# Products with V in three blocks of columns for two units instead of two for one, and the sums copied a unit later

## What is computed

```python
scores = jnp.einsum('bhqd,bhkd->bhqk', q, k) / math.sqrt(hd)
causal = jnp.triu(jnp.ones((S, S), dtype=bool), k=1)
scores = jnp.where(causal[None, None], -jnp.inf, scores)
attn = jax.nn.softmax(scores, axis=-1)
attn_out = jnp.einsum('bhqk,bhkd->bhqd', attn, v)
```

## Time and profile before

| | |
|---|---|
| median of 3 runs | 2348.08 us (2337.51 to 2354.03) |
| the profiled execution | 2345.42 us, span 2343.7 us |
| first maximum job to last product with V | 378 to 1919 us of the span |
| first scores to last product with V | 464 to 1919 us |
| PE, DVE, ACT busy in the span | 95%, 83%, 62% |

### The profile page before, as it was taken

The page is one execution under the profiler, slowest core; times in us unless marked ns, Lnnn a source line. Parts: engine busy times, 40 slices in busy tenths (PEclk is TensorE's granted clock), DMA queues, the critical chain, the costliest instruction groups (busy, mean ns, idle before and its releaser), DMA issues. The chain is left out here.

```text
span 2343.7 us, 48214 instructions
## 1 busy us (share of the span) xinstructions
PE 2221.6 (95%) x18596; PEld 1346.0 (57%) x18596; DVE 1955.3 (83%) x3662; ACT 1460.4 (62%) x1759; POOL 216.2 (9%) x287
## 2 busy tenths in 40 slices
PE   0999997999999999999999999999999989999998
PEld 0888984444444454444444444444444438998998
DVE  8788786979989989999899989899888826777887
ACT  1444440077767777777777778778778775555443
POOL 3111111010020310000000000000000000000544
PEclk9999996589989999999999999999999999999999
DMA  5223327111110120210001111000200016443232
GB/s 141 86 95 125 121 94 144 39 34 35 34 44 17 60 62 2 66 34 12 22 11 34 34 49 55 22 14 10 31 19 8 4 37 191 154 149 103 80 99 81
DMA packets 138310, 143.67 MB, mean 61 GB/s; under 512 B 36184, under 2 KB 101336, under 8 KB 137992
## 3 DMA queue, kind: packets, MB, share of 16 engines
q1 hardware_dynamic: 134784, 132.56, 20.0%
q0 software_dynamic: 3072, 8.39, 1.1%
q10 hardware_dynamic: 288, 0.39, 0.1%
HBM read 88.17 MB, written 51.02 MB: 59 GB/s over the span
## 5 line engine op out<-in xcount | busy, mean ns | idle before, releaser
L1048 DVE TENSOR_REDUCE attn_MX<-psB 128x1 f32<-128x512 f32 (+3 forms) x2176 | 1331.9, 670 | 160.9 <-PE psB L862 98.0
L1021 ACT ACTIVATE attn_PB<-psB 128x1024 f32<-128x1024 f32 (+3 forms) x1152 | 1076.3, 954 | 383.1 <-PE psB L916 314.3
L862 PE MATMUL psB<-KS,attn_QS 52*128 52x512 f32 (+3 forms) x1152 | 331.9, 457 | 25.1 <-DMA KS<-picking_rows 16.1
L938 PE MATMUL psB<-attn_PB,V 128*32 128x256 f32 (+4 forms) x4008 | 338.6, 410 | 0.0
L938 PE MATMUL psB<-attn_PB,attn_V 128*32 128x256 f32 (+5 forms) x3552 | 320.6, 433 | 0.5 <-ACT attn_PB L1021 0.4
L916 PE MATMUL psB<-attn_QS,KS 52*128 52x512 f32 (+3 forms) x1152 | 285.1, 473 | 0.1
L862 PE MATMUL psB<-attn_KS,attn_QS 52*128 52x512 f32 (+3 forms) x1152 | 279.6, 405 | 3.1 <-DVE attn_MX L1048 1.9
L916 PE MATMUL psB<-attn_QS,attn_KS 52*128 52x512 f32 (+3 forms) x1152 | 273.6, 461 | 4.8 <-ACT attn_PB L1021 3.8
L862 PEld LDWEIGHTS psB<-KS,attn_QS 52*128 52x128 f32 x1152 | 192.7, 201 | 94.6 <-DVE attn_MX L1048 67.5
L916 PEld LDWEIGHTS psB<-attn_QS,attn_KS 52*128 52x128 f32 x1152 | 111.3, 183 | 228.3 <-issue 116.7
L916 PEld LDWEIGHTS psB<-attn_QS,KS 52*128 52x128 f32 x1152 | 114.6, 187 | 218.4 <-issue 145.8
(11 more groups left out here) (232 smaller groups left out, 3102.4 us busy)
## 6 DMA issues: line engine op xcount, KB each, us to landing
W<-in_w SPq DMA_DIRECT2D x18, 1024.0 KB, 5.4
qk_parts<-proj_PT SPq DMA_DIRECT2D x32, 512.0 KB, 2.8
attn_QS<-qk_parts SPq DMA_DIRECT2D x192, 64.0 KB
v_rows<-proj_VA SPq DMA_DIRECT2D x32, 256.0 KB, 2.0
attn_KS<-qk_parts SPq DMA_DIRECT2D x96, 64.0 KB, 2.8
KS<-qk_parts SPq DMA_DIRECT2D x90, 64.0 KB, 3.2
XN<-in_x SPq DMA_DIRECT2D x8, 512.0 KB, 7.5
rows_by_place<-proj_ZR SPq DMA_DIRECT2D x32, 128.0 KB, 2.2
```

The costliest lines, as they stand in the source:

```text
L862: mm = nc.tensor.matmul(ps[:, bank, at * width:(at + 1) * width], QS[rows, i % 4, b, j * P:(j + 1) * P], KS[w][rows, b, kc * CH:kc * CH + ...
L938: mm = nc.tensor.matmul(ps[32 * h:32 * (h + 1), PV, cols], V[w][:, kb, 32 * h:32 * (h + 1)], PB[:, u % RING, h, cols], start=(k == 0 and f ...
L1021: nc.scalar.activation(PB[:, u % RING, 2 * pair:2 * pair + 2, r * P:CH], ps[:, 2 * (s % 2):2 * (s % 2) + 2, r * P:CH], ACT.Exp, scale=HD * ...
L1048: nc.vector.tensor_reduce(MX[:, m % 4, first:first + 2 * n - 1:2, kc], ps[:, MB + off % 3, 0:n * w].rearrange("p (h n) -> p h n", h=n), AX ...
```

## The change

PE's order is now written for two units a and b together, with the two units before them (`behind`) weighed in three blocks of columns. For eight new jobs in a pair of units it is: first scores of a, 3 jobs, block one; second scores of a, 1 job, first scores of b, 1 job, block two; second scores of b, 3 jobs, block three. Blocks are cut at a third and two thirds of all columns of both units, so the middle block has a part of each unit, with its own matmuls. The last two units are weighed whole at the end. ACT copies the sums of the step before after the second unit of a step instead of after the first. In steps with only four units SP moves the rows of maxima before it stores the sums.

```diff
+                    rows_first = i + 1 < LS and len(units[i]) == TPC
+                    if rows_first:
+                        move_rows(i + 1)
                     if i > 0:
                         sp.wait_ge(ou_ready, i + 1)
                         store_sums(i - 1)
...
-                    if i + 1 < LS:
+                    if i + 1 < LS and not rows_first:
                         move_rows(i + 1)
...
-                        scores(i, k, 0)
-                        ask(done + (2 if halves else (new + 1) // 2))
-                        if halves:
-                            mid = (units[behind[0]][behind[1]][1] * P + CH) // 2
-                            weigh(*behind, 0, mid)
-                        scores(i, k, 1)
...
-                        ask(done + 4 if halves else upto[i][k])
-                        if behind is not None:
-                            weigh(*behind, mid if halves else 0, CH)
...
+                    widths = [CH - P * units[i][k][1] for i, k in two]
+                    ends = [sum(widths) * q // 3 // 16 * 16 for q in range(3)] + [sum(widths)]
+                    for (i, k), base, width in zip(two, (0, widths[0]), widths):
+                        first, last = [min(max(end - base, 0), width) for end in ends[third:third + 2]]
+                        if first < last:
+                            weigh(i, k, CH - width + first if first > 0 else 0, CH - width + last)
...
+                    share = lambda q: at + ((of_b - at) * q + 4) // 8
+                    first, second = min(share(3), of_a), max(share(5), of_a)
+                    both_scores(*a, 0)
+                    ask(first)
+                    weigh_third(behind, 0)
+                    both_scores(*a, 1)
+                    ask(of_a)
+                    both_scores(*b, 0)
+                    ask(second)
+                    weigh_third(behind, 1)
+                    both_scores(*b, 1)
+                    ask(of_b)
+                    weigh_third(behind, 2)
...
-                        if k == 0 and i > 0:
+                        if k == 1 and i > 0:
                             sums(i - 1)
```

More of the change, by code:

```diff
@@ L959, in _ @@
                             max_rows(0, 0, None, 1)
-                behind = None
+                flow = [(i, k) for i in range(LS) for k in range(len(units[i]))]
                 at = j_base[AHEAD]
@@ L968, in ask @@
                         at += 1
[L970 to L974, removed]
-                        scores(i, k, 0)
-                        ask(done + (2 if halves else (new + 1) // 2))
-                        if halves:
-                            mid = (units[behind[0]][behind[1]][1] * P + CH) // 2
-                            weigh(*behind, 0, mid)
-                        scores(i, k, 1)
-                        if k == rows_at(i) and i + 1 < LS:
-                            max_rows(i + 1, s_rows(i), s_rows(i) - 1, i + 2)
-                        ask(done + 4 if halves else upto[i][k])
-                        if behind is not None:
-                            weigh(*behind, mid if halves else 0, CH)
[L986 to L989, removed]
@@ L990, in _, with both_scores, weigh_third @@
-                weigh(*behind, 0, CH)
+                def both_scores(i, k, pair):
+                    scores(i, k, pair)
+                    if pair == 1 and k == rows_at(i) and i + 1 < LS:
+                        max_rows(i + 1, s_rows(i), s_rows(i) - 1, i + 2)
+                def weigh_third(two, third):
+                    if not two:
+                        return
+                    widths = [CH - P * units[i][k][1] for i, k in two]
[4 more added lines that the diff above has]
+                            weigh(i, k, CH - width + first if first > 0 else 0, CH - width + last)
@@ new lines, in _ @@
+                for n in range(0, len(flow), 2):
+                    a, b = flow[n:n + 2]
+                    behind = flow[max(n - 2, 0):n]
+                    of_a, of_b = upto[a[0]][a[1]], upto[b[0]][b[1]]
+                    share = lambda q: at + ((of_b - at) * q + 4) // 8
[11 more added lines that the diff above has]
+                    weigh_third(behind, 2)
+                    if a == (LS - 1, 0):
+                        transposes()
@@ L992, in _ @@
+                for i, k in flow[-2:]:
+                    weigh(i, k, 0, CH)
             @block.scalar
```

## The result

The changed kernel takes 2536.24 us (median of 4 runs, 2523.21 to 2547.78) against 2344.58 us before: a ratio of 1.082, 95% interval 1.078 to 1.086. I had forecast slower, 2480 us, with a range up to 2525. The direction was right and so was the mechanism at the joints; the size was too small by 56 us, and the next sections find what was missing. Times are medians of all runs; clocks, half-clock times and lines are those of the profiled execution.

The account below looks back on a forecast made before the run. PE sets the pace, with DVE near, and waits for banks at joints should decide: 36 + 35 + 37 + 23 = 131 us on the profiled 2345.4 us, forecast 2480 us. Its own range is 2450 to 2510, over all 2415 to 2525.

Parts of the forecast that it names:

- joint of six: Six jobs around only block three, at joints between pairs: job n waits for job n-3's reduce; 190 of 287 joints.
- The price of a joint: Full pairs cannot repeat faster than 5.49 us: 0.47 us more with eight or nine jobs, 0.71 with seven.
- PE's own order: PE's work for a pair without bank waits: 4.89 us, against 5.02 before with eight jobs and 4.78 with seven.
- The diagonals and the rest: 65 joints in pairs touching a diagonal, 0.56 us each, 37 us; 97 pairs without clump, 0.24 us each, 23 us.
- ACT at nothing: Exponentials of b wait for the middle block's first part; 2 us of PE work covers them, costed at nothing.
- waits that end with ACT's L1041: Listed sign, in the changed profile, that the forecast is wrong: waits ending with ACT's line L1041.
- Rival 4: New pauses halve PE's clock for a tenth of the scores' stretch: up to 145 us more, about 2600; chance 0.04.
- Rivals 1 and 2: 1: PE's own work stays the bound, about 2341 us, chance 0.05; 2: the clump costs half, 2420 us, chance 0.12.
- Rival 3: ACT waits too, at the joints, its cover short by 0.1 us: 29 us more, 2509 us; chance 0.12.

Follow-up runs that it names:

- first unit in middle: Changed kernel with the second column cut never before the end of the first unit, so the middle block always finishes it: 2475.94 us, ratio 1.060.
- and rows later: Changed kernel with the middle block always finishing the first unit, and the rows of maxima placed behind the pair's jobs: 2438.22 us, ratio 1.043.
- and even jobs: Changed kernel with the middle block finishing the first unit, rows of maxima behind the pair's jobs, and two jobs in each place: 2379.31 us, ratio 1.014.
- four-block kernels: Changed kernel with each unit weighed in halves, four blocks per pair: 2395.11 us with two jobs per place, 2913.99 us with jobs placed 3, 1, 1, 3.
- DVE made cheap: Maxima over half of a job's columns, exponential scale a hundredth: 2325.1 us on the kernel "first unit in middle", 2266.9 us on the kernel before.

## Why the prediction was half right

Where the time over the kernel before lies, worked out from the starts of the scores in the traces, pair of units by pair of units (us; "full" are pairs of full units with neither a diagonal nor the rows of maxima in them or in the pair that they weigh, a stricter count than the forecast's):

| pairs | forecast | the change | first unit in middle | and rows later | and even jobs |
|---|---|---|---|---|---|
| full, joint of six, 8 or 9 jobs | 36 (76 pairs) | 29 (68) | 30 | 28 | 25 |
| full, joint of six, 7 jobs | 35 (49) | 25 (37) | 28 | 25 | -1 |
| others with a joint of six | 37 (65) | 94 (85) | 62 | 37 | 10 |
| no joint of six | 23 (97) | 40 (97) | 11 | 3 | -2 |
| sum | 131 | 188 | 131 | 93 | 31 |

**The price of a joint: right.** 5.49 us forecast for a pair of eight or seven; the mean of full pairs at full clock is 5.47 for eight and 5.42 for seven. Per full pair this gives 0.43 and 0.67 us over before, where I had 0.47 and 0.71. The four-block kernels show the mechanism from the other side, at 6.16 us against 6.2.

**PE's own order: right in kind.** 4.83 measured with DVE made cheap, 4.89 worked out, for eight and for seven alike; that a pair of seven can't gain was foreseen.

**The diagonals and the rest: right by luck where they have no pauses.** 37 us for the joints there is what the kernel with the pauses taken out shows, over more joints at a smaller price each; the 97 pairs without a clump were priced at 23 us and cost 3. With both pauses and most of the clock out, the change costs 93 us and not 131.

**ACT at nothing: the step that failed.** I wrote that PE has 2 us of work between the middle block's first part and its need of the exponential. That holds for two units of 512 columns. It fails where the first unit has 512 columns and the second 128 (the first then ends in block three), and before the rows of maxima, where one pair of scores is all that lies between. I checked the cover in the middle of a step and not at its two ends. The pauses themselves are 30 us. Net of what the pairs beside them gain or lose, the first kind is worth some 9 us and the rows' place some 26. Of my signs of being wrong, "waits that end with ACT's L1041" is the one that came.

**The clock at a chance of 0.04: the other failure, and the dearer one.** Rival 4 came true: the time at half clock rose by 169 us, 160 of them inside attention, and the clock there was 0.94 and not near 0.99. I argued that a busy share of 88% would keep the clock up since 79% did in the first stretch. A share over a long stretch did not tell it: the fall shown above came 1.35 us behind the second of two pauses of half a microsecond near each other, in a stretch that was 90% busy. The Trainium skill, "TensorE: Matmul & The Clock Gate", "A second HAM failure mode: psum-queue depth-cycling", tells of a kernel whose short pauses between groups of matmuls let the clock swing between its two levels. The runs here agree, with 0.937 against 0.962 for one edit that removes such a pause and 0.958 for one that fills it. At 0.36 us for each microsecond at half clock the 160 us are worth some 58.

So the 188 us are, within 2 us: 93 for joints and PE's order, some 35 for the pauses with what hangs on them, and some 58 for the clock. My 131 had an excess of 38 in the first and nothing of the other two.

**Rivals 1 and 2** (PE's own work the bound; the clump costs half) are refuted by the pairs of 5.47 us. **Rival 3** (ACT waits at the joints, 29 us): at the joint of full units shown above PE has no idle time that ends with ACT; the long waits for ACT lie at the ends of steps.

What stays open: which pauses the clock falls behind and which not, why some falls have no idle time of PE over 0.15 us in the 6 us before them (one of 30.7 us in the kernel with the first unit in the middle block, two of 3.4 us in the kernel before), and why clumps alone bring the clock down with four blocks and not with three.

## What to carry to other kernels

Where one engine fills n buffers in turn for another that is nearly as busy, count how many fills stand between two long pieces of other work: beyond n, the filler waits for the other engine, which had stood idle before them, and spreading the same fills evenly gives that back (here 59 us of 2438). When an edit is costed at nothing because other work covers it, check the cover at the ends of a stage with its odd sizes, not in its middle. And price pauses of a matmul engine twice: once as time, and once for what they may do to its clock; here some 58 us against some 35.

## What was unexpected of the hardware

- TensorE's granted clock fell to 0.5 within 1.4 us behind pauses of 0.56 and 0.48 us, with PE otherwise busy, and stayed there for 37.5 us even though PE's records then show it busy for 37.46 of them. Stretches at half clock inside attention last 3 to 58 us in the kernels with such pauses. In the four-block kernel with the clump, which has no such pauses, they last 27 to 358 us.
- Filling a pause with products by zeros made the kernel 38 us faster.
- A microsecond at half clock cost 0.36 us in two kernels as different as 2536 and 2914 us, in a loop that PE and DVE bound together. A loop of PE's work alone, at half speed, would lose 0.50.
